# Sigmoid rounding moved from ScalarE to GpSimd in the gated up stage of a two-layer transformer kernel

## The reference

```python
def act_qdq(x):
    scale = jnp.maximum(jnp.max(jnp.abs(x)) / 32767.0, 1e-12)
    return jnp.clip(jnp.round(x / scale), -32768.0, 32767.0) * scale

def fixed_qdq_u16(x):
    return jnp.clip(jnp.round(x * 65536.0), 0.0, 65535.0) / 65536.0
...
up = act_qdq(x @ lpbq_dequant(w_up).T)
gate = act_qdq(x @ lpbq_dequant(w_gate).T)
sig = fixed_qdq_u16(jax.nn.sigmoid(gate))
gate = act_qdq(gate * sig)
o = act_qdq(gate * up)
return o @ lpbq_dequant(w_down).T
```

## Time and profile before

| | us |
|---|---|
| median of the runs | 620.23 |
| the profiled execution, its own time | 621.77 |
| its span on the engines | 620.0 |
| TensorE busy | 520.9 (84%) |
| VectorE busy | 391.9 (63%) |
| ScalarE busy | 289.9 (47%) |
| GpSimd busy | 152.7 (25%) |

### The profile page before, as it was taken

The page is one execution under the profiler, slowest core; times in us unless marked ns, Lnnn a source line. Parts: engine busy times, 40 slices in busy tenths (PEclk is TensorE's granted clock), DMA queues, the critical chain, the costliest instruction groups (busy, mean ns, idle before and its releaser), DMA issues.

```text
span 620.0 us, 9446 instructions
## 1 busy us (share of the span) xinstructions
PE 520.9 (84%) x3298; PEld 368.2 (59%) x3298; DVE 391.9 (63%) x943; ACT 289.9 (47%) x557; POOL 152.7 (25%) x218
## 2 busy tenths in 40 slices
PE   0869999799899700599999999998499999999994
PEld 0548866644344300487757677776366777777673
DVE  5665689845479979868789799986623322233101
ACT  1526668723399958400258788884021122212220
POOL 2705535000000000000223223211114445344531
PEclk9969999999999955699999999999599999999998
DMA  7900000000000000250000011015105354444410
GB/s 226 294 0 2 1 2 1 2 0 1 0 0 0 1 0 1 77 195 1 1 1 1 2 35 36 2 36 168 16 23 189 118 196 135 164 147 156 132 43 21
DMA packets 31993, 37.57 MB, mean 61 GB/s; under 512 B 8656, under 2 KB 27728, under 8 KB 31952
## 3 DMA queue, kind: packets, MB, share of 16 engines
q1 hardware_dynamic: 28880, 29.07, 14.4%
q0 software_dynamic: 3072, 7.95, 4.4%
HBM read 30.14 MB, written 6.88 MB: 60 GB/s over the span
## 4 chain that ended last, share of the span: by engine, by line
PE 61%; DVE 22%; issue 7%; ACT 6%; DMA 1%; SPq 1%; DVEq 1%; POOLq 0%; POOL 0%; ACTq 0%
PE pA L1814 11%; PE pB L1832 9%; PE pC L1544 6%; DVE rm L1178 5%; PE pA L1506 4%; PE pC L1506 3%; PE pB L1506 3%; PE pA L1576 3%; DVE arena L1187 3%; ACT arena L585 2%; PE pC L1418 2%; DVE arena L1096 2%; PE pC L1825 2%; PE pB L1329 2%; PE pA L1399 1%
## 5 line engine op out<-in xcount | busy, mean ns | idle before, releaser
L464 POOL TENSOR_TENSOR arena<-KT,par 128x256 f32<-128x256 f32 x32 | 19.0, 614 | 263.2 <-DVE arena L1116 200.5
L1814 PE MATMUL pA<-arena 128*128 128x320 f32 x256 | 74.1, 438 | 0.9 <-ACT arena L780 0.9
L787 ACT ACTIVATE arena<-pA 128x320 f32<-128x320 f32 x64 | 28.0, 437 | 71.8 <-PE pA L1814 71.8
L1832 PE MATMUL pB<-arena 128*128 128x256 f32 x256 | 59.3, 385 | 0.0
L1814 PEld LDWEIGHTS pA<-arena 128*128 128x128 f32 x256 | 47.4, 190 | 19.4 <-issue 1.1
L1832 PEld LDWEIGHTS pB<-arena 128*128 128x128 f32 x256 | 47.4, 190 | 9.4 <-issue 3.1
L1029 DVE TENSOR_REDUCE am<-arena 128x1 f32<-128x512 f32 (+1 forms) x48 | 32.0, 680 | 22.5 <-ACT arena L622 22.5
L1544 PE MATMUL pC<-wdnT,arena 128*128 128x256 f32 x192 | 42.9, 381 | 1.8 <-DVE arena L1116 1.8
L1544 PEld LDWEIGHTS pC<-wdnT,arena 128*128 128x128 f32 x192 | 36.0, 190 | 7.8 <-DVE arena L1116 2.8
L1582 PE MATMUL pC<-ident,arena 128*128 128x128 f32 x256 | 37.7, 279 | 2.7 <-DVE arena L1172 1.2
L1329 PE MATMUL pB<-ident 128*128 128x128 f32 x80 | 14.0, 353 | 30.2 <-DVE arena L1096 30.2
(11 more groups left out here) (311 smaller groups left out, 1118.1 us busy)
## 6 DMA issues: line engine op xcount, KB each, us to landing
arena<-in_L_ffn_wi SPq DMA_DIRECT2D x8, 1024.0 KB, 5.4
arena<-in_L_ffn_wo SPq DMA_DIRECT2D x8, 1024.0 KB, 5.9
X<-in_x SPq DMA_DIRECT2D x4, 512.0 KB, 6.0
arena<-in_ctx SPq DMA_DIRECT2D x4, 512.0 KB, 5.8
out<-X SPq DMA_DIRECT2D x4, 512.0 KB, 3.0
token_rows<-arena SPq DMA_DIRECT2D x4, 512.0 KB, 6.6
arena<-in_L_ffn_w_up SPq DMA_DIRECT2D x1, 768.0 KB, 9.2
arena<-in_L_ffn_w_gate SPq DMA_DIRECT2D x1, 768.0 KB, 10.6
```

Source lines behind the costliest of these rows:

```text
L1814: last = mm(ps[2 + f % 2][:, 0:ROWS], WI[:, u, k, f * P:(f + 1) * P], XET[:, u, k, :], start=(k == 0), stop=(k == KD - 1))
L1832: last = mm(ps[4 + c][:, 0:D], HT[:, u, f, c * P:(c + 1) * P], WO[:, u, f, :], start=(f == 0), stop=(f == NFT - 1))
```

## The change

The odd gate rows are no longer turned into integers by VectorE; ScalarE does all sixteen, into a `GI` of four buffers, two rows ahead of the sigmoid. Of the four rows of a chunk, the first (row 4c) is rounded to uint16 by ScalarE as before, into a single `SI` buffer that now lies in the weight tile `wgtT`, whose gate weights are done with. The other three are rounded by GpSimd: it adds 192 to the float32 sigmoid in `SG`, in place. Between 128 and 256 a float32 has steps of 1/65536, so the sum is rounded to such a step; a minimum with 192 + 65535/65536 clips it. VectorE's product is now one `scalar_tensor_tensor`, which subtracts the 192 (or scales `SI` by 1/65536) and multiplies by `GI`. ScalarE may write the sigmoid of row b into `SG` once the product of row b - 2 is done. One scalar operation on `sc` (line 1049) falls away. Matmuls, evacuations and maxima stay as they are.

```diff
-        SI = tiles(F3, 2, U16)
-        GI = tiles(F3, 3, I16)
+        GI = F3[:, 1536:3072].bitcast(I16).rearrange("p (u f n) -> p u f n", u=4, f=FT)
+        SI = wgtT[:, 0, 0:FT * P // 2].bitcast(U16).rearrange("p (f n) -> p f n", f=FT)
...
+            def sig_round(b, u):
+                pool.wait_ge(s["sig"], b + 1)
+                nc.gpsimd.tensor_scalar(SG[:, u], SG[:, u], SIXTEENTH, SIXTEENTH + 65535.0 / 65536.0, ALU.add, ALU.min).then_inc(s["sig_round"], 1)
+            for b in range(NB):
+                if b % 4:
+                    sig_round(b, b % 2)
...
             def g_to_int(b, u):
-                free_after(act, s["gs_done"], b)
-                nc.scalar.activation(GI[:, u], F_b(G, b), ACT.Copy, scale=sc[:, 7:8]).then_inc(s["g_int0"], 1)
+                if not isinstance(b, int) or b >= 4:
+                    act.wait_ge(s["gs_done"], b - 3)
+                nc.scalar.activation(GI[:, u], F_b(G, b), ACT.Copy, scale=sc[:, 7:8]).then_inc(s["g_int"], 1)
+
+            def sigmoid(b, u, early):
+                act.wait_ge(s["g_int"], b + 1)
+                if not early:
+                    act.wait_ge(s["gs_done"], b - 1)
+                nc.scalar.activation(SG[:, u % 2], GI[:, u], ACT.Sigmoid, scale=sc[:, 5:6]).then_inc(s["sig"], 1)
...
                 for f in range(FT):
+                    if f < 4:
+                        sigmoid(4 * c + f, f, first and f < 2)
                     evacuate(U, "up", c, f)
+                    if f == 0:
+                        act.wait_ge(s["sig"], 4 * c + 1)
+                        nc.scalar.activation(SI[:, :, :], SG[:, 0], ACT.Copy, scale=65536.0).then_inc(s["sig_int"], 1)
+                    if f < 4 and not (final and f >= 2):
+                        g_to_int(4 * c + f + 2, (f + 2) % 4)
...
-            def gate_sig(b, u):
-                dve.wait_ge(s["sig_int"], b + 1)
-                V_.tensor_tensor(F_b(G, b), GI[:, u], SI[:, u], ALU.mult).then_inc(s["gs_done"], 1)
+            def gate_sig(c, j):
+                if j == 0:
+                    dve.wait_ge(s["sig_int"], c + 1)
+                    V_.scalar_tensor_tensor(out=F_b(G, 4 * c), in0=SI[:, :, :], scalar=1.0 / 65536.0, in1=GI[:, 0], op0=ALU.mult, op1=ALU.mult).then_inc(s["gs_done"], 1)
+                else:
+                    dve.wait_ge(s["sig_round"], 3 * c + j)
+                    V_.scalar_tensor_tensor(out=F_b(G, 4 * c + j), in0=SG[:, j % 2], scalar=-SIXTEENTH, in1=GI[:, j], op0=ALU.add, op1=ALU.mult).then_inc(s["gs_done"], 1)
...
             def up_chunk(c):
                 for j in range(4):
-                    if j % 2 == 0:
-                        g_to_int(4 * c + j + 1, 1)
-                    gate_sig(4 * c + j, j % 2)
+                    gate_sig(c, j)
```

More of the change, by code:

```diff
@@ L18 @@
 ROUND = 12582912.0
+SIXTEENTH = 192.0
 QMAX = 32767.0
@@ L634, in g_to_int @@
             def g_to_int(b, u):
-                free_after(act, s["gs_done"], b)
-                nc.scalar.activation(GI[:, u], F_b(G, b), ACT.Copy, scale=sc[:, 7:8]).then_inc(s["g_int0"], 1)
+                if not isinstance(b, int) or b >= 4:
[6 more added lines that the diff above has]
+                nc.scalar.activation(SG[:, u % 2], GI[:, u], ACT.Sigmoid, scale=sc[:, 5:6]).then_inc(s["sig"], 1)
             def up_chunk(c):
+                first = isinstance(c, int) and c == 0
+                final = isinstance(c, int) and c == 3
                 for f in range(FT):
[L641 to L649, removed]
-                    evacuate(U, "up", c, f)
[L651 to L656, removed]
+                    if f < 4:
+                        sigmoid(4 * c + f, f, first and f < 2)
+                    evacuate(U, "up", c, f)
+                    if f == 0:
[3 more added lines that the diff above has]
+                        g_to_int(4 * c + f + 2, (f + 2) % 4)
             g_to_int(0, 0)
+            g_to_int(1, 1)
             up_chunk(0)
@@ L1047, in _ @@
             link(V_.reciprocal(sc[:, 9:10], sc[:, 5:6]))
[L1048 to L1053, removed]
-            def gate_sig(b, u):
-                dve.wait_ge(s["sig_int"], b + 1)
-                V_.tensor_tensor(F_b(G, b), GI[:, u], SI[:, u], ALU.mult).then_inc(s["gs_done"], 1)
+            V_.tensor_scalar(sc[:, 7:8], sc[:, 9:10], sc[:, 0:1], None, ALU.mult).then_inc(s["sc_gate"], 1)
+            def gate_sig(c, j):
[5 more added lines that the diff above has]
+                    V_.scalar_tensor_tensor(out=F_b(G, 4 * c + j), in0=SG[:, j % 2], scalar=-SIXTEENTH, in1=GI[:, j], op0=ALU.add, op1=ALU.mult).then_inc(s["gs_done"], 1)
             def gs_max(b):
@@ L1082, in _ @@
             gs_all, up_all = ps[0][:, 256:257], ps[0][:, 257:258]
-            link(V_.tensor_scalar(sc[:, 15:16], gs_all, sc[:, 14:15], 1.0 / QMAX, ALU.mult, ALU.mult))
+            link(V_.tensor_scalar(sc[:, 15:16], gs_all, sc[:, 5:6], 1.0 / QMAX, ALU.mult, ALU.mult))
             link(V_.tensor_scalar(sc[:, 2:3], up_all, sc[:, 0:1], 1.0 / QMAX, ALU.mult, ALU.mult))
@@ L1089, in _ @@
             link(V_.reciprocal(sc[:, 8:9], sc[:, 4:5]))
-            link(V_.tensor_scalar(sc[:, 10:11], sc[:, 16:17], sc[:, 14:15], None, ALU.mult))
+            link(V_.tensor_scalar(sc[:, 10:11], sc[:, 16:17], sc[:, 5:6], None, ALU.mult))
             V_.tensor_scalar(sc[:, 6:7], sc[:, 8:9], sc[:, 0:1], None, ALU.mult).then_inc(s["sc_up"], 1)
```

## The result

The changed kernel takes 622.33 us (median of 8 runs, 621.54 to 623.12), the kernel before 620.45 in the same sessions: ratio 1.0036, interval 1.0024 to 1.0049. It is slower by 1.9 us by the medians and 2.2 by the ratio, where 3.5 less were forecast.

What follows compares the result with a forecast made beforehand. VectorE was taken to pace the up stage at 11.79 us a chunk; less 1.32 of conversions leaves 10.47, so with a late first row the stage ends 3.5 us earlier, median 620.23 to 616.7, range 616.0 to 631.5.

Steps and rivals of the forecast that it cites:

- What bounds, and what is left on VectorE: Up stage: VectorE paces it at 11.79 us a chunk; without two conversions (1.32) 10.47 are left.
- The product's form: VectorE's product in the up stage: 0.95 us for 768 columns in the new form, as before; no change taken.
- R: Length of GpSimd's rounding of a 768-column row in the up stage: taken as 1.3 us, bounds 0.74 and 2.6.
- the exclusion between a rounding and a product: GpSimd rounding and VectorE product, both on SBUF: exclude each other, but with a short R lie beside each other anyway.
- The sentence on the Trainium skill: GpSimd's rounding: 1.03 cycles per element give an estimated 0.66 us before dispatch, the sum 0.5 us better; not adopted.
- Rival one: Up stage: GpSimd and VectorE shut each other out, R long; slower, 628.0 at R = 2.3, some 631.5 at 2.6; chance 0.31.
- it stood until a GpSimd instruction ended: Reading of VectorE's line 831, 0.407 us with GpSimd idle and 0.810 while it ran: waited out the whole GpSimd instruction.
- Rival two: Same exclusion in the up stage, R between 1.4 and 1.8; some products lose the race: 617.5 to 623.5; chance 0.16.
- The sum: Up stage: first chunk ends at 186.0, three chunks of 10.47 follow, end at 218.4 instead of 221.9: 3.5 us less.
- The spare time in the loop: Up stage's loop of sigmoid, rounding and product: nothing waits in a circle, 0.7 us to spare before row 3's sigmoid.
- 0.37 for slower: Whole kernel: chance given to a slower result, beside 0.53 for faster by over 0.2% and 0.10 for same.
- its lowest third: GpSimd's rounding in the up stage: R up to 1.4, the forecast's own case, 616.0 to 617.6, chance 0.43.

Runs made afterwards that it cites:

- e1: Changed kernel with GpSimd rounding only 128 of a row's 768 columns, the rest left unrounded; ratio to the kernel before 0.9931.
- e6: Changed kernel with four sigmoid buffers instead of two; ratio to the kernel before 0.9988, interval 0.9975 to 1.0002.
- e2: Changed kernel with GpSimd only adding 192, the minimum left out; ratio to the kernel before 1.0009.
- e4: Changed kernel with GpSimd rounding rows 1 and 3 of a chunk and ScalarE rows 0 and 2; ratio to the kernel before 1.0001.
- e8: Kernel before, with 18 two-operation tensor_scalar on unused columns keeping GpSimd busy beside the up stage; ratio to the kernel before 1.0030.
- e7: Changed kernel with three GpSimd memsets of a row in place of each rounding; ratio to the kernel before 0.9944.
- e10: Changed kernel, two sigmoid buffers, with ScalarE converting row 1 and taking its sigmoid before row 0 in chunk 0; ratio to the kernel before 1.0045.

## Why the prediction was wrong

**What bounds, and what is left on VectorE: right.** 10.47 us a chunk without the conversions is what e1 and e6 measured in their best chunk. The product's form costs nothing more (0.94 to 0.96), and in the changed kernel VectorE stands for neither ScalarE nor TensorE after product 0.

**The length of a rounding: the step that failed, by its size.** I took R = 1.3, and it measured 2.77. With it failed the term that hung on it: with a short R I put the exclusion between a rounding and a product at nothing, and it cost 4.0 us. The one row on GpSimd's tensor_scalar was line 487, 0.863 for 256 columns and one operation. I let a memset's 0.96 ns a column stand for the rest, and put 0.6 of the 0.863 down as fixed. e2's 2.13 for 768 columns says (2.13 - 0.863) / 512 = 2.5 ns a column and 0.23 fixed; the tensor_tensor row's pace, 2.9 ns, which I had beside it, was nearer. The second operation adds 0.84 ns a column. By both, 0.23 + 768 x 3.3 ns = 2.77, and e1's 128 columns come to 0.65, where 0.64 was measured.

The sentence on the Trainium skill (GPSIMD Engine Reference, section 3.1) leaned further the same way: its 1.03 cycles per element are an estimated 0.66 us, and the measured 3.3 ns are four cycles of 1.2 GHz. The measurement decides. (With 0.66 the sum would have been 0.64 better, not the 0.5 given.)

**How GpSimd and VectorE exclude each other: the rival had the wrong mechanism.** Rival one let a rounding shut a product out for its whole length and priced R = 2.6 at 631.5; the result lies 9 us below, because only the first part excludes. (Its sum for R = 2.3 has a slip: 3 x 1.6 + 3.7 - 0.5 is 8.0 and not 7.8.) By the changed kernel's trace, e2, e4 and e8, the product is held until 0.70 after a rounding's start, by e1 0.16 at 128 columns; by e7, memsets, which only write, don't hold it. The earlier trace rows could not tell this, since line 970 only met GpSimd's start. The trace behind the earlier trace rows could: line 831's operations that start at 22.90, 23.63 and 24.37 each end 0.93 after the start of a GpSimd instruction (22.78, 23.52, 24.26; 0.77 to 0.78 long). Had they stood to its end and then taken their 0.41, they would have ended 1.19 after it. So "it stood until a GpSimd instruction ended" was read wrongly. Rival two's "no change in the middle of it" lies near the result by luck: it wants R between 1.4 and 1.8, and races that some products lose by the whole rounding.

The Trainium skill (SBUF — State Buffer, Who interferes with whom) says that two SBUF inputs contend with a GpSimd instruction that reads SBUF and not with one that only writes; e7 and e8 bear that out. It also says the first holds the pair for the whole instruction, and there the runs differ: 0.70 of 2.77, with the product running beside the rest.

**The sum, mended.** From the forecast's stage of 50.27 (53.77 - 3.5): product 1 comes 4.53 after product 0 and not 3.23, +1.30; the stretched products 1 and 2 of chunk 0, 0.62 and 0.43, +1.05; in each of three chunks 0.13 + 0.43 + 0.43 = 0.99, +2.97; product 0 lies 0.21 earlier in the stage, -0.21. Together 55.38, as measured. No run shows that the 0.21 comes from the change: seven runs with the changed kernel's code up to there (e1 to e7) have 6.44 or 6.45 where it has 6.29, and e8, with the code of the kernel before, has 6.44. Of the 5.1 us between, 4.0 are stretched products, of which the forecast had none, and 1.3 the longer first wait. Both come with the long rounding, but not in proportion: at 0.64 (e1) nearly nothing is stretched, at 2.13 (e2) as much as at 2.77. No run has a rounding of 1.3, so whether the forecast's own R would have kept clear of the stretches isn't shown.

**The spare time in the loop.** I had left 0.7 us before anything waits in a circle. With 2.77 ScalarE stands 0.50 before two sigmoids of a chunk, yet no product after the first waits for GpSimd; e2 shows that the loop is held by the stretches, not by R.

**The chances.** 0.37 for slower was too little. R was open between 0.74 and 2.6 and I gave 0.43 to its lowest third, which only a memset's pace supported.

## What to carry to other kernels

Before moving an elementwise operation to GpSimd, price it from GpSimd's own rows of that operation, both its fixed part and its cost per column and per operation. A row of one size doesn't give the slope.

Then look at when it starts, not only at how long it runs: a GpSimd instruction that reads holds up VectorE's operations with two SBUF operands at its beginning. If its start is released by a VectorE operation of a fixed time before, the two meet in every turn of the loop; more buffers between the engines loosen that, as two more buffers did here for 2.7 us of the stage.

An engine added to a line of engines costs its latency once, as lag, and three ways of starting elsewhere didn't save it here. Against a gain of 1.3 us a chunk it must be counted.

## What the runs showed of the hardware

- GpSimd's tensor_scalar on float32: 2.13 us for 768 columns with one operation, 2.77 with two, 0.64 for 128 with two: 0.2 fixed, 2.5 and 3.3 ns a column.
- A product of two SBUF operands on VectorE is kept out by a reading GpSimd instruction for its first 0.16 us at 128 columns and 0.70 at 768, whatever the operands' types (float32 with int16, uint16 with int16), and then runs at full speed beside it. Reductions were never longer (0.67 to 0.69 for 512 columns and 0.93 to 0.95 for 768 in every run). Of eight conversions with one operand beside a busy GpSimd (e8), two took 1.02 and 1.08 instead of 0.61.
- GpSimd's memsets, 0.74 each, lengthened no product and no reduction (e7). In the other direction a GpSimd instruction of 2.77 is made longer when VectorE is in such a product at its start: 3.25 in e8, 3.50 in e10, where the product had begun 0.07 before it.
